# A new table of times for the order of all steps in a fused cross-attention and mixture kernel on one core

## The reference, cut to what matters

```python
x = x + tanh(g_xattn[0]) * mixer(ctx, ctx, layernorm(x), ssm_kernel, D)      # per head: sum_i conv(k_i * v_j) * q_i
x = x + tanh(g_ffn[0]) * experts(layernorm(x), gate_w, mask_up, gate, up, down)
...
x = x + tanh(g_xattn[1]) * attention(layernorm(x), ctx, mask)
x = x + tanh(g_ffn[1]) * ternary_mlp(layernorm(x), w_fc, w_proj)             # square(relu(x @ T(w_fc))) @ T(w_proj)
```

## Time and profile before

| | |
|---|---|
| median of 3 runs | 254.12 us (253.78 to 254.71) |
| the profiled execution | 252.56 us |
| its span, first to last instruction | 250.8 us |
| TensorE busy | 228.7 us (91%) |
| VectorE busy | 183.5 us (73%) |
| ScalarE busy | 107.9 us (43%) |
| GpSimd busy | 83.1 us (33%) |
| mean granted clock of TensorE | 0.98 |

### The profile page before, as it was taken

The page is one execution under the profiler, slowest core; times in us unless marked ns, Lnnn a source line. Parts: engine busy times, 40 slices in busy tenths (PEclk is TensorE's granted clock), DMA queues, the critical chain, the costliest instruction groups (busy, mean ns, idle before and its releaser), DMA issues.

```text
span 250.8 us, 4672 instructions
## 1 busy us (share of the span) xinstructions
PE 228.7 (91%) x1602; PEld 217.3 (87%) x1602; DVE 183.5 (73%) x513; ACT 107.9 (43%) x221; POOL 83.1 (33%) x126
## 2 busy tenths in 40 slices
PE   6795899798789999999999999999999999999985
PEld 5694789687669989998989989999899999999784
DVE  2379999998997799687887576752774844676664
ACT  2430364542104353664535555563341772364233
POOL 5588898078797601000355001100100000111110
PEclk9997999999899999999999999999999999999979
DMA  5799752000000041000000000000001001000101
GB/s 175 208 353 222 227 148 86 0 1 3 1 0 0 3 142 70 0 1 3 0 0 3 0 0 4 0 4 0 0 3 42 3 0 43 3 0 0 44 1 42
DMA packets 14055, 11.50 MB, mean 46 GB/s; under 512 B 2929, under 2 KB 13777, under 8 KB 14033
## 3 DMA queue, kind: packets, MB, share of 16 engines
q1 hardware_dynamic: 13936, 11.16, 14.8%
q10 hardware_dynamic: 96, 0.05, 0.1%
HBM read 10.14 MB, written 1.07 MB: 45 GB/s over the span
## 4 chain that ended last, share of the span: by engine, by line
issue 43%; PE 28%; POOL 13%; DVE 9%; DMA 4%; ACT 1%; ACTq 0%; SPq 0%; POOLq 0%; DVEq 0%
PE bank L695 9%; PE bank L545 4%; POOL fold L1318 4%; PE bank L552 4%; POOL rstd L1287 3%; DMA ring<-in_gate_p 2%; PE bank L596 2%; POOL kv L1307 2%; POOL fold L1321 2%; PE bank L598 2%; PE bank L597 2%; POOL tern_tmp L1294 2%; PE bank L698 1%; PE bank L766 1%; DMA lags<-in_kernel_rev 1%
## 5 line engine op out<-in xcount | busy, mean ns | idle before, releaser
L695 PE MATMUL bank<-w_split,xt 128*128 128x352 f32 x384 | 68.7, 328 | 0.7 <-DVE act L1195 0.6
L695 PEld LDWEIGHTS bank<-w_split,xt 128*128 128x128 f32 x384 | 60.9, 188 | 1.2 <-issue 1.2
L1283 POOL TENSOR_SCALAR ve<-mv 128x2 f32<-128x2 f32 (+2 forms) x16 | 3.7, 234 | 135.9 <-DVE mv L985 135.9
L1195 DVE SCALAR_TENSOR_TENSOR act<-silu,scal,bank 128x176 f32<-128x176 f32 x64 | 22.4, 392 | 19.3 <-ACT silu L891 17.3
L545 PE MATMUL bank<-d_split,a_t 128*128 128x256 f32 x264 | 33.6, 285 | 0.0
L545 PEld LDWEIGHTS bank<-d_split,a_t 128*128 128x128 f32 x264 | 32.3, 191 | 0.3 <-DVE a_t L946 0.2
L891 ACT ACTIVATE silu<-bank 128x352 f32<-128x352 f32 x32 | 14.8, 464 | 29.4 <-PE bank L698 29.3
L1318 POOL TENSOR_TENSOR fold<-prod 128x256 f32<-128x256 f32 x32 | 25.2, 787 | 5.7 <-DVE prod L1032 3.9
L775 ACT ACTIVATE a_t<-bank 128x384 fp32r<-128x384 f32 (+1 forms) x32 | 14.7, 461 | 18.7 <-PE bank L552 18.6
L1307 POOL TENSOR_TENSOR kv<-ctx_ext 128x640 f32<-128x640 f32 x16 | 20.2, 1269 | 4.1 <-PE bank L598 2.1
L596 PE MATMUL bank<-kv,toe 128*128 128x160 f32 x64 | 16.0, 334 | 5.8 <-issue 3.0
(11 more groups left out here) (141 smaller groups left out, 434.1 us busy)
## 6 DMA issues: line engine op xcount, KB each, us to landing
toe<-lag_rows SPq DMA_DIRECT2D x4, 512.0 KB, 7.5
ring<-in_down_p SPq DMA_DIRECT2D x2, 704.0 KB, 4.5
ctx<-in_ctx_rows SPq DMA_DIRECT2D x2, 512.0 KB, 5.0
ring<-in_gate_p SPq DMA_DIRECT2D x2, 512.0 KB, 6.5
ring<-in_up_p SPq DMA_DIRECT2D x2, 512.0 KB, 7.4
out_x<-x_res SPq DMA_DIRECT2D x3, 256.0 KB, 2.2
tern_w<-in_w_fc SPq DMA_DIRECT2D x1, 640.0 KB, 4.3
tern_w<-in_w_proj SPq DMA_DIRECT2D x1, 640.0 KB, 5.5
```

The lines of the kernel that those rows point to most:

```text
L695: pe.matmul(psum((name, b, c))[:, 0:CW], lhs, w_split[:, w, kt, part, cols], start=i == 0, stop=False)
L1195: drain(dve.scalar_tensor_tensor(out=act[:, g * NI:(g + 1) * NI], in0=silu[:, n % 2, cols], scalar=scal[:, b, g:g + 1], in1=psum(("up", b, ...
```

## The change

All numbers of `TIMES` are new, and so is the place of nearly every step. The chains, their inner order and every instruction stay. Two details are part of it: `KEEPS` grows from 10 to 13 products, and four of the eight keeps now stand early in the list; and since the banks are planned along the list, steps can get another bank by the same rules.

```diff
-KEEPS = [1, 1, 1, 2, 1, 2, 1, 1]
+KEEPS = [1, 1, 1, 3, 3, 1, 1, 2]
 TIMES = {
-    "keeps": [1229, 1260, 1272, 1272, 1272, 1272, 1272, 1272],
...
-    "kv0": [43, 70, 79, 108, 159, 196],
+    "kv0": [-940, -581, -263, -157, 37, 50],
...
+    "keeps": [-291, -285, -201, -173, 1291, 1436, 1448, 1734],
...
```

More of the change, by code:

```diff
@@ L64 @@
 WARMS = [8, 7, 0]
-KEEPS = [1, 1, 1, 2, 1, 2, 1, 1]
+KEEPS = [1, 1, 1, 3, 3, 1, 1, 2]
 TIMES = {
-    "keeps": [1229, 1260, 1272, 1272, 1272, 1272, 1272, 1272],
-    "weights": [39, 76, 84, 94, 144, 158, 158, 227, 247, 247, 247, 265, 276, 281, 294, 312, 315, 315, 317, 338, 373,
-        373, 373, 373, 387, 452, 466],
-    "consts": [97],
[9 rows of a table removed]
[L80 to L86, removed]
[9 rows of a table removed]
+    "weights": [-656, -459, -215, -134, 35, 46, 100, 125, 144, 178, 178, 189, 244, 244, 247, 275, 289, 313, 344,
+        377, 378, 419, 455, 486, 487, 487, 539],
+    "consts": [-9],
[9 rows of a table added]
+    "mask": [799],
+    "ternary": [678, 745, 815, 839, 849, 864, 887, 916, 928, 948, 984, 1005, 1022, 1041],
+    "chunks": [531, 545, 559, 604, 638, 680, 721, 721, 737, 748, 775, 799, 822, 825, 853, 878, 893, 908, 964, 983,
+        1003, 1015, 1015, 1033, 1039, 1056, 1069, 1109, 1123, 1143, 1177, 1183],
+    "turns": [560, 578, 601, 677, 702, 724, 733, 755, 792, 804, 838, 868, 888, 895, 910, 942, 948, 994, 1011, 1023,
+        1030, 1036, 1042, 1067, 1077, 1097, 1116, 1136, 1167, 1175, 1181, 1197],
+    "downs": [687, 795, 889, 942, 1024, 1076, 1156, 1210],
+    "keeps": [-291, -285, -201, -173, 1291, 1436, 1448, 1734],
[9 rows of a table added]
 }
```

## The result

| | before | changed |
|---|---|---|
| median of its runs, us | 253.95 (253.05 to 254.71) | 245.82 (245.73 to 247.52, 4 runs) |
| ratio, 95% interval | | 0.9707 (0.9665 to 0.9750) |
| profiled execution: time, span, us | 252.56, 250.8 | 245.73, 244.0 |
| TensorE busy, share of the span | 91% | 93% |
| first chunk / start of down 7, us | 73.62 / 224.26 | 71.38 / 219.18 |

The changed kernel is 2.9% faster by the ratio of the runs (3.2% by the two medians). A repeat gave 245.81 us and a ratio of 0.9698 (0.9665 to 0.9731).

The account below looks back on a forecast made before the run. What decides: when VectorE ends router 0, which starts the chunks, and the last batch's chain. -5.0 + 0.8 + 0 - 1.2 = -5.4 us gave 247.2, plus 1.56 a median of 248.7 us; 8-in-10 range 246.2 to 252.3.

Parts of the forecast that it names:

- Part 1: Ahead of router 0 on VectorE: work moved behind soft 0 and idle time removed, net -5.0 us (-3.3 to -6.9).
- I take 1.7 us: Up to the first chunk: VectorE idle time expected to go, out of a possible 0 to 3.6 us.
- Soft 0 comes 6.0 us earlier, the first chunk at 67.6: End of router 0: 4.3 us of moved work plus 1.7 us of idle time bring the first chunk forward from 73.62.
- Parts 2 and 3: Chunks beside the mixer's second half: +0.8 us (0 to +4.3) for postponed VectorE work; the middle: 0 (-1 to +1).
- Part 4: Tail: -0.8 us of TensorE work ahead of down 7, earlier scores 4 behind it; -1.2 us in all (0 to -2.8).
- An order can give back 2.2 us there at most: From 93.00 to 228.40 us: TensorE works 133.19 of 135.40 us, which limits what reordering can win.
- The anchor: Whole kernel: the profiled execution lies 1.56 us under the median, so 247.2 becomes a median of 248.7 us.
- Down 7 ends at 223.4: Start of the tail: a sign that the forecast is right; before the change down 7 ended at 228.4 us.
- a first chunk later than 70 us: End of router 0: a sign that the forecast is wrong; between 67 and 68.5 us was expected.
- the first (work only shifted): VectorE stays the bound through the mixer's second half, costing +4 us behind the first chunk; 251.9 us, chance 0.22.
- The second (all goes well): Front idle time gone in full, postponed work free, clock up in the tail; 244.4, halfway 246.5 us, chance 0.12.
- The third and fourth: ScalarE: two added set changes delay silu, 251.3 us, chance 0.05; exp waits delay chunks, 256.5 us, chance 0.05.

Follow-up runs that it names:

- kv12_late: The changed kernel with kv 1 2 moved behind fold 1 0 on GpSimd; 244.82 us, ratio 0.9661.
- keep_top2: The changed kernel with eight keep records ahead of turn_top 0, on the bank turn_top 0 takes next, all later banks unchanged; 245.37 us, ratio 0.9683.
- h_front2: The changed list up to chunk 2 0 (place 187), then all remaining steps in the order of the list before; 252.79 us, ratio 0.9948.
- h_front: The changed list up to the first chunk, then all remaining steps in the order of the list before; 254.82 us, ratio 1.0053.
- no_head_keeps: The changed kernel without keeps 0 to 3 (six products, 12 records near the head); 244.73 us, ratio 0.9665.
- keep_top: The changed kernel with eight more keep products ahead of turn_top 0, which moved the bank rotation by one; 249.05 us, ratio 0.9830.

## Why the prediction was right, and where its sum was not

The sign and the rough size were right, but the parts were not: two large errors of opposite sign nearly cancelled. Against the profiled execution the sum said -5.4 us, and it is -6.8.

**Part 1, the front: -5.0 forecast, -1.3 measured.** The first chunk came 2.24 us earlier, less the 0.95 us of TensorE's work left behind. The half on GpSimd held: kv 0 3 was forecast to end at 19.1 us, conv 0 6 starts at 19.57, and the 3 us gap is gone. soft 0 ends 4.3 us earlier, the size of the work taken out of the way, but partly by luck: 1.3 us of idle time went as well, and longer instructions took about as much back. Two steps of this part failed.
- "I take 1.7 us" of idle time, which put soft 0 6.0 us earlier. 1.3 us of VectorE's idle time did go (4.88 to 3.60 us up to the first chunk), but some durations grew, by 1.6 us on balance: the norm by 0.9 us and the division by 1.0 us beside a kv that the new order had put there, and three of the constants' instructions by some 1.2 us, where before two others had lost 1.5 us. I had priced every VectorE instruction as independent of what GpSimd does. kv12_late shows the stall of the norm and its removal.
- "Soft 0 comes 6.0 us earlier, the first chunk at 67.6" assumed that TensorE follows soft 0 as before. I had seen 0.50 at 67 us and called it cheap because VectorE set the pace. Between flat 0 and turn_soft 0 TensorE's work is about the same as before: 12 turned tiles came in (1.3 us at full clock) and two of four convolutions went out (1.6 us). But soft 0 was 4.3 us earlier, and the clock was at 0.50 for 6.8 us (62.8 to 69.7) instead of 3.4 us (66.6 to 70.0), so the slow TensorE became the later of the two. keep_top2 shows this step: clock up, and the chunk is back at 1.7 us behind soft 0.

**Parts 2 and 3: +0.8 and 0 forecast, together -3.0 measured** (-2.84 to the start of down 7, with the 0.95 us taken off and the 0.8 us of Part 4 ahead of it added, which I take as forecast and have not measured). VectorE's 17.51 us in 21.62 was enough, and the postponed 4.3 us cost nothing there. "An order can give back 2.2 us there at most" was the right bound and then I took 0: the new order gave back nearly all of it, wait by wait. (The other 0.7 us are busy time, for 1,070 records against 1,068 up to the start of down 7; I can't divide it.) I had put the term at nothing because the waits were scattered, and that is no reason when every place in the list may move. With the old middle the waits stay (h_front2). Which move removes which wait was not tested one by one.

**Part 4: -1.2 forecast, -0.4 of it behind down 7, where -1.8 was measured.** The maximum of scores 4 was expected 6.5 us behind the end of down 7 and was there after 6.3 (229.42 + 0.29). The order's share behind down 7 is 0.6 us (20.6 for the 21.2 of the same old tail at full clock), and the other 1.2 us are the clock, which I had put at 1.6 us and not taken. The old tail showed both: 22.4 us at 0.92, and 21.2 and 21.3 at 1.00 in h_front2 and h_front. The new tail took 20.6 us in each of its eleven profiled executions (two of them without its keeps), at clocks of 0.97 to 1.00. So 0.6 us belong to the order; whether the new tail also avoids the fall, or the execution of before was merely one of the slower ones, three executions of the old tail don't decide.

**The anchor.** I added 1.56 us for the distance of the profiled execution from the median. That distance did not carry over: the changed kernel's is 0.1 us. Of the 2.9 us between forecast (248.7) and median (245.8), half is this.

**Down 7 ends at 223.4** was forecast and came out as 219.18 + 4.20 = 223.38, with Part 1 3.7 us too good and Parts 2 and 3 3.8 us too bad. A sum that fits is no proof of its terms; the mark "a first chunk later than 70 us" was what told the error.

**Of the rivals**, the first (work only shifted) needed +4 us behind the first chunk, where the opposite came. The second (all goes well) is nearest to the time, but for another reason than its own: neither the whole idle time nor VectorE's room in the front, but the middle. The third and fourth did not happen: 10 loads ahead of silu for the 9 of before at the same 1283 ns, and one wait of 0.2 us for all the chunks.

**What stays open.** How much of the median's 8.1 us belongs to the clock: only the profiled execution of each run shows where it fell. Some 2 us of the gain appear in neither half by itself, and no run places them. Which moves removed the seven waits of the middle no run tells either. And the best of my versions (no_head_keeps at 244.73, kv12_late at 244.82, each with 4 runs) can't be told from the changed kernel; the two ideas joined gave 245.20, so I claim no better kernel.

## What to carry to other kernels

When the banks are dealt out along the list of steps, moving a step changes who shares a bank with whom, and a step of 0.14 us made TensorE wait 2.4 us at the next chunk and 1.8 us some 12 us later: look, for each bank, at who must have read it before the next writer, and not only at the queues. When you remove work from the engine that sets the pace, price the next engine at the clock that its rows there show (here 0.50), since it can be the next bound. When many small waits are left in a stretch and every place of the list may move, their sum may go: here 2.2 of 2.6 us did. And when two halves of a list are run apart, look at the banks on both sides of the seam before taking the result for what a half is worth.

## What the runs showed of the hardware

- **VectorE stands still beside GpSimd on some instructions.** With all operands in SBUF, the norm's two L1007 took 1.66 us beside a kv and 0.72 us without, and the division took 1.26 or 0.74 us beside a kv (it began 0.13 or 0.66 us into it) and 0.33 us without. Each of the stalled ones ended 0.14 to 0.15 us behind the kv that ran beside it. A fold does the same: before the change L1174 (two inputs in SBUF) took 0.82 us instead of 0.29 and ended 0.14 us behind the fold beside it. The products that read a PSUM bank did not change (32 of L1028 between 0.456 and 0.492 us), nor did the sum L1041, with its one input in SBUF (16 between 0.669 and 0.686 us). The Trainium skill ("GPSIMD Engine Reference", section 1, Specifications) says that GpSimd's SBUF interfaces are shared with VectorE, with contention for VectorE instructions in a 2-port mode or with two SBUF inputs. The trace agrees for the division, which has two inputs in SBUF, and for the two that did not change, which have at most one. Whether the norm, with one large input, falls under the first condition, no run here shows.
- **Whether and when the clock falls can differ between executions of one list.** The same old tail had 0.92 in one execution and 1.00 in two others, worth 1.2 us. Ahead of the first chunk the clock fell near 62.8 us in one profiled execution of the changed kernel and at 65.5 in the next. What stayed the same there is that it fell: in all eight profiled executions in which TensorE had waited 1.9 to 2.0 us for rt ahead of turn_top 0, it fell behind that wait, 0.3 to 2.3 us after turn_top 0 began. With the eight products in that wait (keep_top, keep_top2) it stayed at 1.00 up to the first chunk.
- **Loads arrive unevenly.** In ten profiled executions whose lists are the same up to that point, TensorE got the first of the up weights between 28.75 and 31.40 us, after waiting 1.3 to 4.4 us for it; with the list of before it was 28.27 in one execution and 29.88 in another. A difference of some 2 us at the first chunk can't be read without looking at them.
